# Moving one VectorE product from turn 7 to turn 6 in a fused Mamba and mixture-of-experts layer

## The chip, the cores and the metric

The kernel runs on one core of a Trainium2 chip, in one launch. The metric is the device time in microseconds, the median of several executions. All data is float32.

## The reference

Input x has 2 sequences of 2048 tokens with 256 features. Two blocks follow each other, each on a layer norm of its input and with a residual:

```python
x = x + _L0_attn_ref(_layernorm(x), ...)   # Mamba, then a gated feed-forward of 1024/2
x = x + _L0_ffn_ref(_layernorm(x), ...)    # 8 experts of rank 128, the best 2 of each token count
```

The first holds a state-space scan with 512 channels and 16 states, `h = h * dA + dt * B * x`, `y = sum over states of h * C`. The second, which the change touches:

```python
rw, selected_experts = jax.lax.top_k(routing_weights, TOP_K)
...
combine = jnp.sum(jax.nn.one_hot(selected_experts, N_EXPERTS) * rw[..., None], axis=1)
for e in range(N_EXPERTS):
    out = out + combine[:, e, None] * (x @ Wa[e] @ Wb[e])
```

## The kernel before, in words

The 4096 tokens are cut into 16 tiles of 256 tokens, called steps here and numbered 0 to 15 in their order: (c, b) is chunk c of sequence b, and the two sequences alternate. Each step goes through five stages: `enter` (first norm, input projection, convolution of 4 taps), `ready` (step sizes dt, B and the scan's inputs), `main` (the scans over 16 states), `back` (gate, output projection, feed-forward) and `tail` (router and experts). The stages of different steps are laid over each other: one iteration has 16 turns, one for each state s of the step that is in `main`; around it, in the same turn s, every other stage does its own piece s for another step. So one iteration works on up to five steps, and a step's tail runs two iterations after its scans. The code of all five engines is written in this one order by `drive` (line 147): in a turn first `main(s, n, 0)`, then the four stage functions in an order given for each engine, then `main(s, n, 1)`. Each engine runs its own list in order, and semaphores hold it where it needs another. An opening and a closing list do the turns for which there is no whole iteration; the iterations whose scans are those of chunks 2 to 5 are a loop of two iterations a round.

`main` on VectorE (line 964): `main(s, n, 0)` makes two scans of 128 x 256 (line 975), `main(s, n, 1)` the other two. They read dA (from ScalarE, line 796), psx (PSUM, filled by TensorE from bxT at line 1184) and the state before. GpSimd multiplies the four results with C (hC, line 570), and TensorE sums them over the states in PSUM (line 1203), two turns later. psx has three banks, so TensorE's fill for (turn s + 1, first half) must wait for the scans of (turn s - 1, second half), and a fill of a second half for the scans of (turn s, first half).

The experts in `tail`: the combine weights `cw` become `cT` by a TensorE transpose (line 1297) and a ScalarE copy (line 878, turn 5). SyncE stores cT to DRAM (line 446) and loads it back onto all 128 partitions as `cbc`, 8 experts x 256 tokens (line 450, 1 MB written). TensorE's `hidden(i)` (lines 1320 to 1329) makes x @ Wa of experts 2i and 2i + 1 in the PSUM tile pst, in turns 6, 7, 8 and 9; it waits for the product before, since pst holds one pair. VectorE multiplies this pair by its weights in place, in cbc (line 1031), in turns 7, 8, 9 and 10, and counts `hE_done`. Turns 12 to 14 make the product with Wb. The first product waits for the landing of cbc.

Other work near these turns. VectorE: in turn 6 the output projection's residual x1 and its statistics (lines 991, 907, 912) and two taps of the convolution (line 948, four instructions, `enter`), in turn 7 the last tap (two instructions); in turn 8 `sp_l` (line 956) and `sp_e` (958) of the softplus, in turn 9 its line 962, from which GpSimd makes dt (line 542) and then adds the convolution's edge to `acc` (line 534); ScalarE makes `xc` from it (line 701), then the silu of `sz` (823) and the second gate `yg` (809), for which TensorE waits in turn 10. GpSimd: in turn 6 xn (line 510), in turn 7 nx (line 483), which TensorE transposes in turn 8 (line 1054, called from 1241). TensorE in turn 7 also makes the gate inputs (line 1158), which wait for the last tap.

Steps 12 and 13 have their tails in the iterations where no new step enters, so no taps lie in these turns; steps 14 and 15 have theirs in the closing.

Of the kernel before, what the change touches and what calls it, by code (L numbers as in the profile page):

```python
# [52 lines left out]
def count(per_step, step, k):  # L53

    c, b = step
    value = c * (2 * per_step) + (per_step * b + k)
    return max(value, 0) if isinstance(value, int) else value
# [53 lines left out]
def opening():  # L111

    a, b = (0, 0), (0, 1)

    def turns(stage, step, *at):
        return [(stage, s, step) for s in at]

    return (turns("enter", a, *range(11), 13, 14, 15) + turns("ready", a, 0, 1, 2) + turns("enter", a, 11, 12)
            + turns("ready", a, 5, 6) + turns("enter", b, 0, 1, 2, 3) + turns("ready", a, 7, 8)
            + turns("enter", b, 4) + turns("ready", a, 9) + turns("enter", b, 5) + turns("ready", a, 10)  # L120
            + turns("enter", b, 6, 7, 8, 9, 10) + turns("ready", a, 12, 13, 14, 15)
            + turns("enter", b, 11, 12, 13, 14, 15))


def closing():

    a, b = (NC - 1, 0), (NC - 1, 1)

    def turns(stage, step, *at):
        return [(stage, s, step) for s in at]  # L130

    return (turns("back", b, 0, 1) + turns("tail", a, 0, 1) + turns("back", b, 2, 3) + turns("tail", a, 2, 3)
            + turns("back", b, 4) + turns("tail", a, 4, 5) + turns("back", b, 5, 6, 7)
            + turns("tail", a, 6, 7, 8, 9, 10) + turns("back", b, 8, 9, 10, 11) + turns("tail", a, 12)
            + turns("back", b, 12, 13, 14) + turns("tail", a, 13, 14, 15) + turns("back", b, 15)
            + turns("tail", b, *range(S)))
# [10 lines left out]
def drive(eng, order, enter, ready, main, back, tail):  # L147

    def iteration(t, k, n, r, e):
        stages = {"enter": (enter, e), "ready": (ready, r), "back": (back, k), "tail": (tail, t)}
        for s in range(S):
            if n:
                main(s, n, 0)
            for name in order[s] if s in order else order["else"]:
                stage, step = stages[name]
                if step:
                    stage(s, step)  # L160
            if n:
                main(s, n, 1)

    def pair(c):
        iteration((c - 1, 0), (c - 1, 1), (c, 0), (c, 1), (c + 1, 0))
        iteration((c - 1, 1), (c, 0), (c, 1), (c + 1, 0), (c + 1, 1))

    stages = {"enter": enter, "ready": ready, "back": back, "tail": tail}
    for name, s, step in opening():
        stages[name](s, step)  # L170
    iteration(None, None, (0, 0), (0, 1), (1, 0))
    iteration(None, (0, 0), (0, 1), (1, 0), (1, 1))
    pair(1)
    with eng.Fori(2, NC - 2) as c:
        pair(c)
    pair(NC - 2)
    iteration((NC - 2, 0), (NC - 2, 1), (NC - 1, 0), (NC - 1, 1), None)
    iteration((NC - 2, 1), (NC - 1, 0), (NC - 1, 1), None, None)
    for name, s, step in closing():
        stages[name](s, step)  # L180


def mamba_moe(nc, x, params, w_in, w_x, w_dt, w_out, w_ff, w_fo, w_a, w_b, w_r, bc_scratch, cw_scratch, out):
# [9 lines left out]
    with ctx:  # L193
# [156 lines left out]
        def tail_fill(name, m):  # L350
            units = LAST_TAIL_UNITS if is_last(m) else TAIL_UNITS
            return count(len(units), m, units.index(name) + 1)
# [11 lines left out]
        def wa_bank(i, m):  # L364
            return (psx[0], psx[1], psx[2], psf)[i] if is_late(m) else pst
# [518 lines left out]
        def _(dve):  # L884
# [13 lines left out]
            def link(which, m, ins):  # L898

                chain, per = chains[which]  # L900
                links[which] = links[which] % per + 1
                ins.then_inc(chain, 1)
                dve.wait_ge(chain, count(per, m, links[which]))
# [105 lines left out]
            def tail(s, m):  # L1009
                b = m[1]  # L1010
                if s == 2:
                    dve.wait_ge(filled_tail, tail_fill("rt", m))
                    dve.wait_ge(rn_done, count(1, m, 1))
                    for j in range(SUB):
                        last = nc.vector.tensor_scalar(lg[:, j, :], pst[:, 0, j * NE:(j + 1) * NE], rn[:, j:j + 1], None,
                                                       ALU.mult)
                    last.then_inc(lg_done, 1)
                    dve.wait_ge(lg_done, count(1, m, 1))
                    link("tail", m, nc.vector.reduce_max(mx[:, :], lg[:, :, :], X))
                    nc.vector.tensor_tensor(lgm[:, :, :], lg[:, :, :], mx[:, :].unsqueeze(2).to_broadcast([P, SUB, NE]),  # L1020
                                            ALU.subtract).then_inc(lgm_done, 1)
                if s == 4:
                    dve.wait_ge(psel_done, count(1, m, 1))
                    link("tail", m, nc.vector.reduce_sum(den[:, :], psel[:, :, :], X))
                    nc.vector.reciprocal(rden[:, :], den[:, :]).then_inc(rden_done, 1)
                if s in (7, 8, 9, 10):
                    i = s - 7
                    dve.wait_ge(filled_tail, tail_fill(f"wa{i}", m))
                    if i == 0:
                        dve.wait_ge(cbc_loaded, count(16, m, 16))  # L1030
                    nc.vector.tensor_tensor(cbc[:, 2 * i:2 * i + 2, :], cbc[:, 2 * i:2 * i + 2, :],  # L1031
                                            wa_bank(i, m)[:, :, :], ALU.mult).then_inc(hE_done, 1)
                if s == 15:

                    dve.wait_ge(filled_tail, tail_fill("wb", m))
                    nc.vector.tensor_tensor(x2[:, b], x2[:, b], pst[:, :, :], ALU.add).then_inc(fin_done, 1)

            drive(dve, {"else": ("back", "tail", "ready", "enter")}, enter, ready, main, back, tail)

        @block.tensor  # L1040
        def _(pe):
# [338 lines left out]
```

## Time and profile before

| | |
|---|---|
| median of 3 runs | 1344.15 us (1343.28 to 1348.33) |
| the profiled execution, its own time | 1344.57 us |
| its span | 1342.8 us, 24275 instructions |
| mean granted TensorE clock | 0.982 of full |
| busy TensorE / VectorE / ScalarE / GpSimd | 1225.4 / 999.9 / 1038.2 / 1085.2 us |
| chain that ended last | PE 66%, DVE 9%, issue 5%, ACT 5%, DMA 4%, POOL 2% |

In the profile PE is TensorE's matmuls, PEld its weight loads, DVE VectorE, ACT ScalarE, POOL GpSimd, SP or SPq SyncE with its DMA queue. L1031 is line 1031 of the kernel. Busy time is what an engine's instructions took; "idle before" is the time an engine stood before an instruction, and behind `<-` is what ended it. Instructions of one engine overlap by up to 0.1 us, so that in a run of them the starts count.

### The profile page before, as it was taken

How to read it: one execution, taken by the hardware profiler on the slowest of the kernel's cores; microseconds unless marked ns; L12 is line 12 of the kernel's file. 1: busy time of each engine (PE TensorE's matmuls, PEld its weight loads, DVE VectorE, ACT ScalarE, POOL GpSimd, SP SyncE). 2: the span in 40 equal slices, each digit the busy share in tenths (PEclk: the TensorE clock that was granted, in tenths of full speed). 3: DMA queues.
4: the chain of work that ended last, by engine and by line, in shares of the span. 5: the costliest groups of instructions: out<-in, count | busy, mean ns of one | idle time of the engine just before them, and what ended most of it. 6: DMA issues, size and time to landing. Idle time of an engine off the chain costs nothing.

```text
span 1342.8 us, 24275 instructions
## 1 busy us (share of the span) xinstructions
PE 1225.4 (91%) x7680; PEld 1053.2 (78%) x7680; DVE 999.9 (74%) x1781; ACT 1038.2 (77%) x2505; POOL 1085.2 (81%) x826
## 2 busy tenths in 40 slices
PE   4586889999999999999999999999999999998986
PEld 3365778887878888788888878788887888887875
DVE  2487979778786977879697787969788796878521
ACT  3789888788777978878787887879798787878320
POOL 3389899898888988888898988888898987889621
PEclk8889999999999999999999999999999999999998
DMA  1411111121121111112111121212021021211001
GB/s 66 174 48 41 47 31 66 41 74 47 39 80 45 60 41 53 61 49 80 50 56 41 60 66 36 80 48 69 28 80 48 32 72 48 72 48 64 17 32 48
DMA packets 29223, 75.08 MB, mean 56 GB/s; under 512 B 3104, under 2 KB 15776, under 8 KB 26528
## 3 DMA queue, kind: packets, MB, share of 16 engines
q1 hardware_dynamic: 29088, 73.41, 16.4%
q8 instruction: 69, 1.13, 0.3%
q14 instruction: 66, 0.54, 0.1%
HBM read 64.61 MB, written 4.59 MB: 52 GB/s over the span
## 4 chain that ended last, share of the span: by engine, by line
PE 66%; DVE 9%; issue 5%; ACT 5%; DMA 4%; POOL 2%; DVEq 0%; ACTq 0%; SPq 0%; POOLq 0%
PE psx L1184 11%; PE psy L1203 11%; PE pst L1067 8%; PE psb L1061 7%; PE psb L1067 7%; DVE h L975 4%; PE pst L1061 4%; PE psf L1061 3%; DMA cbc<-cw_scratch 3%; PE psf L1152 2%; PE psf L1104 2%; PE psf L1093 2%; PE psb L1158 2%; PE psf L1158 1%; ACT dA L796 1%
## 5 line engine op out<-in xcount | busy, mean ns | idle before, releaser
L975 DVE TENSOR_TENSOR_SCAN h<-dA,state,psx 128x256 f32<-128x256 f32 x1024 | 682.5, 727 | 114.9 <-PE psx L1184 95.2
L570 POOL TENSOR_TENSOR hC<-h,bC 128x1024 f32<-128x1024 f32 x256 | 606.5, 2373 | 86.7 <-DVE h L975 79.8
L796 ACT ACTIVATE dA<-dt,neg_a 128x256 f32<-128x256 f32 x1024 | 434.2, 499 | 0.0
L1184 PE MATMUL psx<-ident,bxT 128*128 128x128 f32 x2048 | 305.4, 275 | 27.9 <-DVE h L975 17.1
L1184 PEld LDWEIGHTS psx<-ident,bxT 128*128 128x128 f32 x2048 | 244.5, 142 | 70.4 <-issue 24.9
L784 ACT ACTIVATE bxT<-uTs,BT 128x512 f32<-128x512 f32 x352 | 232.6, 715 | 67.4 <-PE psx L1184 65.9
L1203 PE MATMUL psy<-ident,hC 128*128 128x128 f32 x2048 | 265.5, 273 | 1.5 <-POOL hC L570 1.5
L1203 PEld LDWEIGHTS psy<-ident,hC 128*128 128x128 f32 x2048 | 233.1, 142 | 4.7 <-POOL hC L570 1.7
L554 POOL TENSOR_TENSOR bxT<-uTs,BT 128x1024 f32<-128x1024 f32 x80 | 151.9, 1899 | 26.0 <-PE psx L1184 26.0
L1061 PE MATMUL psb<-nT,w_ff_sb 128*128 128x256 f32 x496 | 121.8, 388 | 12.8 <-ACT yg L809 11.2
L1061 PE MATMUL pst<-eT,w_a_sb 128*128 128x256 f32 x448 | 108.9, 386 | 20.4 <-DVE cbc L1031 20.4
L1061 PEld LDWEIGHTS psb<-nT,w_ff_sb 128*128 128x128 f32 x496 | 89.3, 190 | 34.8 <-ACT yg L809 17.5
L1067 PE MATMUL pst<-w_b_sb,cbc 128*128 128x256 f32 x480 | 110.8, 379 | 0.0
L1061 PEld LDWEIGHTS pst<-eT,w_a_sb 128*128 128x128 f32 x448 | 82.6, 192 | 33.4 <-DVE cbc L1031 22.2
L1067 PEld LDWEIGHTS pst<-w_b_sb,cbc 128*128 128x128 f32 x480 | 90.1, 190 | 11.7
L483 POOL TENSOR_SCALAR nx<-x,mv,rstd 128x256 f32<-128x256 f32 x64 | 77.6, 1222 | 24.4 <-ACT rstd L657 24.4
L948 DVE SCALAR_TENSOR_TENSOR acc<-psf,par,acc 128x255 f32<-128x255 f32 (+1 forms) x180 | 73.9, 474 | 26.2 <-ACT halo L696 26.2
L1067 PE MATMUL psb<-w_out_sb,yg 128*128 128x256 f32 x256 | 63.4, 391 | 2.0 <-ACT yg L836 2.0
L1061 PE MATMUL psf<-uT,w_in_sb 128*128 128x256 f32 x240 | 60.2, 395 | 4.5 <-ACT uT L681 2.5
L542 POOL TENSOR_TENSOR dt<-dt,sp_l 128x1024 f32<-128x1024 f32 x16 | 37.8, 2361 | 30.2 <-DVE sp_l L962 30.2
L803 ACT ACTIVATE state<-h 128x4 f32<-128x4 f32 x256 | 50.5, 203 | 13.3 <-DVE h L975 13.3
L1067 PE MATMUL psb<-w_fo_sb,yg 128*128 128x256 f32 x256 | 60.4, 379 | 0.0
(148 smaller groups left out, 1578.8 us busy)
## 6 DMA issues: line engine op xcount, KB each, us to landing
bC<-bc_scratch SPq DMA_DIRECT2D x64, 512.0 KB, 3.9
cbc<-cw_scratch SPq DMA_DIRECT2D x16, 1024.0 KB, 4.8
xf<-in_x SPq DMA_DIRECT2D x16, 256.0 KB, 2.7
xk<-xn SPq DMA_DIRECT2D x16, 256.0 KB, 4.3
xb<-in_x SPq DMA_DIRECT2D x16, 256.0 KB, 4.3
out<-x SPq DMA_DIRECT2D x16, 256.0 KB, 2.2
w_in_sb<-in_w_in SPq DMA_DIRECT2D x1, 1024.0 KB, 5.1
w_ff_sb<-in_w_ff SPq DMA_DIRECT2D x1, 1024.0 KB, 5.9
```

The source lines that it names most:

```text
L483: last = nc.gpsimd.tensor_scalar(dst[:, j, :], src[:, j, :], mv[k][:, j, 0:1], rstd[k + 1][:, j:j + 1], ALU.subtract, ALU.mult)
L554: nc.gpsimd.tensor_tensor(bxT[:, ring(s)], uTs[:, n[1]], BT[:, n[1], :, s:s + 1].to_broadcast([P, SUB, DI]), ALU.mult).then_inc(bxT_pool, 1)
L570: nc.gpsimd.tensor_tensor(hC[:, s % RC], h[:, ring(s)], bC[:, g % RINGG, s % G:s % G + 1, :].to_broadcast([P, NJ, T]), ALU.mult).then_inc( ...
L784: last = nc.scalar.activation(bxT[:, ring(s), j, :], uTs[:, n[1], j, :], ACT.Copy, scale=BT[:, n[1], j, s:s + 1])
L796: last = nc.scalar.activation(dA[:, s % RA, j, :], dt[:, n[1], j, :], ACT.Exp, scale=neg_a[:, j, s:s + 1])
L803: nc.scalar.activation(state[:, n[1], :, s:s + 1], h[:, ring(s), :, T - 1:T], ACT.Copy).then_inc(state_saved, 1)
L948: nc.vector.scalar_tensor_tensor(out=acc[:, j, tap:], in0=x_bank(i, m)[:, j % 2, 0:T - tap], scalar=pcol(C_CONVW + j * TAPS + k), in1=acc[ ...
L975: last = nc.vector.tensor_tensor_scan(h[:, r, j, :], dA[:, s % RA, j, :], psx[bx_bank(fill)][:, k, :], state[:, b, j, s:s + 1], ALU.mult, ...
L1061: last = mm(dst[:, i, :], w[:, k, c:c + P], rhs[:, k, :], start=k == 0, stop=k == kt - 1)
L1067: last = mm(dst[:, j, :], lhs[:, k, j * P:(j + 1) * P], w[:, k, :], start=k == 0, stop=k == kt - 1)
L1184: last = nc.tensor.transpose(psx[bx_bank(fill)][:, k, j * P:(j + 1) * P], bxT[:, ring(s), j, c:c + P], ident[:, :])
L1203: last = mm(psy[j][:, i * P:(i + 1) * P], hC[:, s % RC, i, j * P:(j + 1) * P], ident[:, :], is_transpose=True, start=False, stop=s == S - ...
```

## The change

VectorE makes the product of the first pair (i = 0) in turn 6, and there as the last of the four stages: behind the two taps of `enter` and ahead of `main(6, n, 1)`. The other three stay in turns 8, 9 and 10. No other engine's list changes.

```diff
@@ -1023,8 +1023,8 @@
                     dve.wait_ge(psel_done, count(1, m, 1))
                     link("tail", m, nc.vector.reduce_sum(den[:, :], psel[:, :, :], X))
                     nc.vector.reciprocal(rden[:, :], den[:, :]).then_inc(rden_done, 1)
-                if s in (7, 8, 9, 10):
-                    i = s - 7
+                if s in (6, 8, 9, 10):
+                    i = max(s - 7, 0)
                     dve.wait_ge(filled_tail, tail_fill(f"wa{i}", m))
                     if i == 0:
                         dve.wait_ge(cbc_loaded, count(16, m, 16))
@@ -1035,7 +1035,7 @@
                     dve.wait_ge(filled_tail, tail_fill("wb", m))
                     nc.vector.tensor_tensor(x2[:, b], x2[:, b], pst[:, :, :], ALU.add).then_inc(fin_done, 1)
 
-            drive(dve, {"else": ("back", "tail", "ready", "enter")}, enter, ready, main, back, tail)
+            drive(dve, {6: ("back", "ready", "enter", "tail"), "else": ("back", "tail", "ready", "enter")}, enter, ready, main, back, tail)
```

On VectorE, in turns 6 and 7 of an iteration in which all stages run. The lines of L975 are the scans (two for a half turn), here with their waits: `bx_filled` is TensorE's fill of psx, `exp_done` ScalarE's dA, `hc_done` GpSimd's hC; `cbc_loaded` is the transfer's landing and `filled_tail` TensorE's `hidden(0)`.

```order
 L948 SCALAR_TENSOR_TENSOR acc<-psf,par,acc 128x254 [waits conv_tap] x2
-L975 SCALAR_TENSOR_TENSOR h<-dA,state,psx 128x256 [waits bx_filled]
-L975 SCALAR_TENSOR_TENSOR h<-dA,state,psx 128x256
-L975 SCALAR_TENSOR_TENSOR h<-dA,state,psx 128x256 [waits state_saved,bx_filled,hc_done,exp_done]
-L975 SCALAR_TENSOR_TENSOR h<-dA,state,psx 128x256
 L1031 TENSOR_TENSOR cbc<-cbc,pst 128x512 [waits cbc_loaded,filled_tail]
+L975 SCALAR_TENSOR_TENSOR h<-dA,state,psx 128x256 [waits bx_filled]
+L975 SCALAR_TENSOR_TENSOR h<-dA,state,psx 128x256
+L975 SCALAR_TENSOR_TENSOR h<-dA,state,psx 128x256 [waits state_saved,bx_filled,hc_done,exp_done]
+L975 SCALAR_TENSOR_TENSOR h<-dA,state,psx 128x256
 L948 SCALAR_TENSOR_TENSOR acc<-psf,par,acc 128x253 [waits conv_tap] x2
```

The product has moved ahead of the four scans of (turn 6, second half) and (turn 7, first half); the last tap, which stood behind the product, stands behind the scans.

On TensorE, in the same turns, before and with the change alike: `hidden(0)`, the fill of psx for the second half of turn 7, the sum over states, the fill for the first half of turn 8, `hidden(1)` and the gate inputs.

```order
L1061 MATMUL pst<-eT,w_a_sb 128x256 [waits cT_done]
L1061 MATMUL pst<-eT,w_a_sb 128x256 x3
L1184 MATMUL psx<-ident,bxT 128x128 [waits scan_done]
L1184 MATMUL psx<-ident,bxT 128x128 x3
L1203 MATMUL psy<-ident,hC 128x128 [waits hc_done]
L1203 MATMUL psy<-ident,hC 128x128 x7
L1184 MATMUL psx<-ident,bxT 128x128 [waits scan_done,bxT_pool]
L1184 MATMUL psx<-ident,bxT 128x128 x3
L1061 MATMUL pst<-eT,w_a_sb 128x256 [waits hE_done]
L1061 MATMUL pst<-eT,w_a_sb 128x256 x3
L1158 MATMUL psf<-w_in_sb,uT 128x512 [waits conv_tap]
```

Nothing moved here. The second fill waits by `scan_done` for the scans that now stand behind the product, and `hidden(1)` behind it by `hE_done` for the product.

## Rows read from the trace of the kernel before

**Rows 1.** The page, busy us (share of the span) x instructions.

```profile
PE 1225.4 (91%) x7680; PEld 1053.2 (78%) x7680; DVE 999.9 (74%) x1781; ACT 1038.2 (77%) x2505; POOL 1085.2 (81%) x826
```

**Rows 2.** Who waited for whom: us in total, times, longest us.

```profile
DVE h L975 <- PE psx L1184: 95.2, 68, 4.6
...
PE pst L1061 <- DVE cbc L1031: 20.4, 14, 2.5
...
DVE cbc L1031 <- DMA cbc<-cw_scratch: 15.8, 6, 7.9
```

**Rows 3.** Order of time, VectorE, step 3: start us, us, instruction, count.

```profile
459.45 1.65 DVE L948 SCALAR_TENSOR_TENSOR acc<-psf,par,acc 128x255 f32<-128x255 f32 x4
461.02 2.65 DVE L975 TENSOR_TENSOR_SCAN h<-dA,state,psx 128x256 f32<-128x256 f32 x4
463.59 0.66 DVE L1031 TENSOR_TENSOR cbc<-cbc,pst 128x512 f32<-128x512 f32 x1
464.17 0.86 DVE L948 SCALAR_TENSOR_TENSOR acc<-psf,par,acc 128x253 f32<-128x253 f32 x2
464.95 2.65 DVE L975 TENSOR_TENSOR_SCAN h<-dA,state,psx 128x256 f32<-128x256 f32 x4
...
468.09 2.66 DVE L956 SCALAR_TENSOR_TENSOR sp_l<-sp_l,ln_one,sp_e 128x1024 f32<-128x1024 f32 x1
```

**Rows 4.** Order of time, TensorE, the same stretch; idle before in brackets.

```profile
459.30 1.89 PE L1061 MATMUL pst<-eT,w_a_sb 128*128 128x256 f32 x8
...
462.45 0.66 PE L1184 MATMUL psx<-ident,bxT 128*128 128x128 f32 x4
464.31 1.99 PE L1061 MATMUL pst<-eT,w_a_sb 128*128 128x256 f32 x8 [1.20 <-DVE cbc L1031]
```

**Rows 5.** Order of time, GpSimd, the same stretch.

```profile
462.56 2.36 POOL L570 TENSOR_TENSOR hC<-h,bC 128x1024 f32<-128x1024 f32 x1 [0.43 <-PE psy L1203]
464.91 2.42 POOL L483 TENSOR_SCALAR nx<-x,mv,rstd 128x256 f32<-128x256 f32 x2
467.30 2.37 POOL L570 TENSOR_TENSOR hC<-h,bC 128x1024 f32<-128x1024 f32 x1
```

**Rows 6.** The transfer of cbc: step 3's issue, and landing of all 16.

```profile
456.48 0.33 SPq L450 DMA_DIRECT2D cbc<-cw_scratch  x1
...
DMA to landing us min/median/max: 4.5/4.8/7.4
```

**Rows 7.** The chain that ended last, step 3, turns 9 and 10.

```profile
474.50 1.82 DVE sp_l L962
...
478.80 0.22 POOL acc L534
...
481.14 0.53 ACT yg L809
...
481.71 1.99 PE psb L1061 x8
```

**Rows 8.** Order of time, VectorE, in steps 2, 4 and 13.

```profile
384.52 0.69 DVE L1031 TENSOR_TENSOR cbc<-cbc,pst 128x512 f32<-128x512 f32 x1 [1.17 <-DMA cbc<-cw_scratch]
...
389.44 1.44 DVE L956 SCALAR_TENSOR_TENSOR sp_l<-sp_l,ln_one,sp_e 128x1024 f32<-128x1024 f32 x1
...
542.54 0.69 DVE L1031 TENSOR_TENSOR cbc<-cbc,pst 128x512 f32<-128x512 f32 x1 [0.28 <-DMA cbc<-cw_scratch]
...
547.07 2.26 DVE L956 SCALAR_TENSOR_TENSOR sp_l<-sp_l,ln_one,sp_e 128x1024 f32<-128x1024 f32 x1
...
1231.98 0.69 DVE L1031 TENSOR_TENSOR cbc<-cbc,pst 128x512 f32<-128x512 f32 x1 [2.60 <-DMA cbc<-cw_scratch]
```

**Rows 9.** Windows: us, busy PE, PEld, DVE, ACT, POOL (x), PEclk, DMA share, GB/s.

```profile
385.30:390.60 5.30, 5.30 (x13) 3.54 (x14) 5.03 (x8) 0.48 (x2) 4.04 (x3) 0.68 0.00 0
...
1232.70:1238.00 5.30, 5.28 (x34) 4.89 (x35) 5.30 (x9) 3.02 (x7) 5.03 (x4) 1.00 0.04 5
```

**Rows 10.** Order of time, TensorE, step 13: the transposes of nx.

```profile
1236.30 0.60 PE L1054 MATMUL psb<-ident,nx 128*128 128x128 f32 x4
```

## The prediction

> **What bounds the kernel now.** I read the page first, then the waits, then the order of time on three engines through one pass of turns 6 to 8, and last the chain of waits. The page gives TensorE 1225.4 us, 91% of the span, and no other engine over 81% [rows 1]: TensorE sets the pace where nothing holds it. The list of waits shows what the change is about: TensorE stood still 20.4 us in 14 waits for VectorE's product of line 1031, and VectorE stood still 15.8 us in 6 such products, waiting for the transfer that fills `cbc` [rows 2].
>
> One pass (the one about 460 us) in detail. VectorE ends the taps of turn 6, starts the four scans of (turn 6, second half) and (turn 7, first half) at 461.02, then the product at 463.59, the taps at 464.17, four scans at 464.95, behind them the second product and line 956 at 468.09; there is no idle time between them [rows 3]. I call S the start of those first four scans (461.02). TensorE ends `hidden(0)` at 459.30 + 1.89 = 461.19, fills psx for the next turn at 462.45, which needs the first two of those scans, and starts `hidden(1)` at 464.31 = S + 3.29, 0.72 behind the product's start, after 1.20 of idling [rows 4]. GpSimd runs hC, nx, hC without a gap [rows 5].
>
> So the change's promise is 1.20 us on TensorE in each pass, and its risk is the scans. Two facts decide. First, the transfer: `cbc` is issued at 456.48 and such a transfer lands 4.5 to 7.4 us later, 4.8 in the median [rows 6], that is at about 461.28, while VectorE reaches the new place at S = 461.02. Second, the chain: in this pass it goes through VectorE's line 962 at 474.50, GpSimd's `acc` at 478.80 and ScalarE's `yg` at 481.14 (behind its `xc` and `sz`) to TensorE's matmul at 481.71 [rows 7]. VectorE's time in turns 7 to 9 is therefore on the path, beside TensorE's, and not cover.
>
> **The change part by part.** Nothing is added or removed: the same 16 products at about 0.66 us, no DMA moves, no queue but VectorE's changes order. One product per token step moves ahead of four scans, so VectorE's work is the same in amount; what changes is where it waits, and what is queued behind the wait. Before, the scans ran while the transfer landed. Now they are behind it. Let P be the product's new start: the later of the landing and the end of `hidden(0)` (461.19), so at least S + 0.2. Behind it: scans at P + 0.58 (464.17 - 463.59 [rows 3]), the first two done at about P + 1.95, TensorE's fill, and `hidden(1)` 0.44 later at P + 2.42. VectorE reaches line 956 at P + 7.07, where it was at S + 7.07.
>
> *TensorE's path*: `hidden(1)` moves from S + 3.29 to P + 2.42, that is by (P - S) - 0.87: earlier by up to 0.67, later if the transfer is late.
>
> *VectorE's path*: everything behind moves by P - S, at least 0.2 later. To this comes line 956, whose length depends on GpSimd: it took 1.44 us where GpSimd had finished its hC, 2.26 in between, and 2.66 where hC ran to 467.30 + 2.37 = 469.67, so 1.58 into it [rows 3, 5, 8]. hC of turn 6 now starts with the later scans, at P + 2.1, and the nx and hC behind it end at P + 9.3, so 2.2 us of line 956 run beside GpSimd, and I put it at 1.44 + 2.2 x (1.22 / 1.58) = 3.1 us, 0.45 more than in the usual pass.
>
> The Trainium skill (SBUF — State Buffer, "Who interferes with whom") says that a VectorE instruction with two SBUF inputs contends with a GpSimd instruction that reads SBUF, and that the loser is blocked fully. By that rule line 956 would lose all 2.2 us and take 3.6, and the sum would be some 6 us higher; the row of 2.66 shows 1.22 lost in 1.58, so I stay with the trace.
>
> Nine usual passes (the products of steps 0, 1, 3, 5, 6, 7, 9, 10 and 11; the product was on time in each). P - S, from each step's rows of issue (like 456.48) plus the median 4.8, less its scan row (like 461.02), is 0.75, 0.2, 0.28, 0.26, 1.1, 2.1, 0.2, 0.43 and 0.4: 5.7 us together. Nine times 0.45 for line 956 is 4.0. VectorE's path has no room in the pass shown (the chain passes from one to the next without a wait for anything else [rows 7]) and up to 0.2 in five others, say 1.0 off. **Sum 8.7.**
>
> Three passes whose product already waited or barely made it (steps 2, 4, 8, with line 948 in them). Step 4's product starts at 542.54 after 0.28 of idling for the transfer, step 2's at 384.52 after 1.17 [rows 8]; P is the same before and after, so the four scans (2.57 us) that hid the transfer now come after it. Less room of 0.3 to 0.5 and with line 956 longer by 0.85, that is 2.9 for step 4, and 2.9 for step 8 the same way. In step 2 TensorE's clock had fallen behind that wait (0.68 of full speed, `hidden(1)` and the matmuls behind it at half of the 2.4 GHz for a while [rows 9]), which already cost the step 1.7, so only 1.3 is left. **Sum 7.1.**
>
> Steps 12 and 13, near the end, have no taps. There too the product waits for the transfer, 2.60 us in step 13 [rows 8], and the scans are now behind it. `hidden(1)` moves from P + 0.74 to P + 2.42; in step 12 another 0.5 comes from the fill behind line 956: 2.2. In step 13 TensorE's transposes of nx stood at 1236.30 = P + 4.32 [rows 10] and nx is now ready at P + 6.9: 2.6. **Sum 4.8.** Steps 14 and 15 (the closing) have no scans between turns 6 and 7: 0.
>
> *The clock*: TensorE's gap before the fill becomes P - S + 0.5, which is 3.2 to 4.4 us in steps 2, 4, 8, 12 and 13. A gap of 2.47 dropped the granted clock to half in step 2 and an equal one did not in step 13, where it stayed 1.00 [rows 9]. Each further drop costs at most what it cost in step 2, 1.7, partly covered by the 0.9 that TensorE's path now has to spare. Bounds 0 and 5 x 1.7 = 8.5; I take 1.5, nearer the lower end, since only one of the two gaps fell.
>
> Total: 8.7 + 7.1 + 4.8 + 1.5 = 22.1 us. The profiled execution took 1344.57, 0.4 above the median of the runs, so the forecast is 1344.6 + 22.1 = **1366.7 us**, 1.6% slower. A measurement of this kernel can tell about 0.5%, 6.7 us, from no change.
>
> **The rivals.** *A: VectorE's path has more room than I read, and only TensorE's counts.* Then nine passes give 5.7 - 9 x 0.87 = -2.1, three give 3 x (2.42 - 0.74) = 5.0 and the last two 3.4: +6.3, or 1350.9 us. For it: the room of up to 0.5 in some passes, and TensorE's own path ends level with ScalarE's at 481.71. Against: the chain of the pass shown runs over VectorE, and line 962 feeds GpSimd directly.
>
> *B, faster: the transfer is there when VectorE comes, and TensorE's wait goes.* If P - S is 0.2 in all 14 passes and TensorE's path alone decides, each gains 0.67: 14 x 0.67 = 9.4, or 1335.2 us. It decides from the point where the landing comes less than 0.87 behind S. For it: in seven of the nine usual passes the landing is that near. Against: five of 14 land 2.7 us or more behind S, as their waits show, and VectorE's path loses in every one.
>
> *C: the clock falls in most of the long gaps, and late landings pile up.* The five at 1.7 each and two more landings at 7 us instead of 4.8 give 22.1 + 7 + 5 = +34, or 1379 us. For it: the gaps are longer than the one that fell. Against: an equal gap stayed at full speed.
>
> *D: the place does not matter*, because a later wait swallows either sign, for one that of the scans for psx, 95.2 us in 68 waits [rows 2], which has time to give: 1344.6. Against: the waits lie behind the point where the two paths meet, with TensorE busy throughout.
>
> **How the numbers follow.** Forecast 0.64, A 0.13, B 0.05, C 0.12, D 0.06. The range leaves out B, D, 0.03 of A and half of C, 0.20 in all: 1349 to 1377. Slower by over 0.5% (above 1351.3) are the forecast, C and 0.05 of A: 0.81. Same: D and 0.08 of A, 0.14. Faster: B, 0.05.
>
> **What would show it.** Right: VectorE's wait for `cbc<-cw_scratch` at line 1031 grows from 15.8 us in 6 waits to about 35 in 14 or more; TensorE's wait at `hidden(1)` for line 1031 goes, and a wait of psx for VectorE's scans takes its place; line 956's mean rises from 2.36 us toward 3. Wrong: the landings come before VectorE; or line 956 stays at 2.66 and `acc` of line 534 no later than before against TensorE, which would be A.

## The result and the profile after

The changed kernel takes 1370.63 us in the median of 4 runs (1369.11 to 1372.81), the kernel before 1344.44: 26 us more. The ratio on record is 1.0188, with a 95% interval of 1.0164 to 1.0212; the recorded ratios, here and below, differ from those of the medians by up to 0.001. The forecast was 1366.7 us in a range of 1349 to 1377. The direction and the size held; two steps of the reasoning did not, and part of the size was luck. All three are named below.

| | before | after |
|---|---|---|
| profiled execution's span | 1342.8 us | 1368.9 us |
| mean granted TensorE clock | 0.982 | 0.975 |
| busy TensorE / VectorE | 1225.4 / 999.9 us | 1234.3 / 1009.7 us |
| line 956, mean | 2.36 us | 2.92 us |

The list of waits of the changed kernel (us in total, times, longest us), against [rows 2]:

```profile
POOL hC L570 <- DVE h L975: 109.6, 67, 4.7
DVE h L975 <- PE psx L1184: 94.4, 68, 4.8
...
PE psx L1184 <- DVE h L975: 54.7, 47, 4.4
...
DVE cbc L1031 <- DMA cbc<-cw_scratch: 31.2, 15, 7.7
```

And the first of these in the kernel before:

```profile
POOL hC L570 <- DVE h L975: 79.8, 61, 3.2
```

TensorE's wait for the product at `hidden(1)` (20.4 us in 14 waits) is gone from the list. In its place TensorE's fill of psx waits 54.7 us for the scans, a wait that had 17.1 us before. VectorE's wait for the transfer doubled, from 15.8 us in 6 waits to 31.2 in 15. GpSimd's wait for the scans grew by 29.8 us, about as much as the kernel; the experiments below bear out that the time goes there.

Step 3 again, in order of time. VectorE, against [rows 3]:

```profile
461.76 1.65 DVE L948 SCALAR_TENSOR_TENSOR acc<-psf,par,acc 128x255 f32<-128x255 f32 x4
464.46 0.69 DVE L1031 TENSOR_TENSOR cbc<-cbc,pst 128x512 f32<-128x512 f32 x1 [1.05 <-DMA cbc<-cw_scratch]
465.06 2.65 DVE L975 TENSOR_TENSOR_SCAN h<-dA,state,psx 128x256 f32<-128x256 f32 x4
467.63 0.84 DVE L948 SCALAR_TENSOR_TENSOR acc<-psf,par,acc 128x253 f32<-128x253 f32 x2
...
471.54 3.27 DVE L956 SCALAR_TENSOR_TENSOR sp_l<-sp_l,ln_one,sp_e 128x1024 f32<-128x1024 f32 x1
```

TensorE, against [rows 4]; the last row is the matmul of turn 10 that waits for `yg`:

```profile
461.61 1.89 PE L1061 MATMUL pst<-eT,w_a_sb 128*128 128x256 f32 x8
...
466.50 0.66 PE L1184 MATMUL psx<-ident,bxT 128*128 128x128 f32 x4 [1.69 <-DVE h L975]
466.99 1.89 PE L1061 MATMUL pst<-eT,w_a_sb 128*128 128x256 f32 x8
...
485.74 1.56 PE L1061 MATMUL psb<-nT,w_ff_sb 128*128 128x256 f32 x6 [0.97 <-ACT yg L809]
```

GpSimd, against [rows 5]:

```profile
466.61 2.37 POOL L570 TENSOR_TENSOR hC<-h,bC 128x1024 f32<-128x1024 f32 x1 [2.11 <-DVE h L975]
468.96 2.44 POOL L483 TENSOR_SCALAR nx<-x,mv,rstd 128x256 f32<-128x256 f32 x2
471.36 2.38 POOL L570 TENSOR_TENSOR hC<-h,bC 128x1024 f32<-128x1024 f32 x1
```

The product is where the order says, and VectorE idles 1.05 us ahead of it for the landing. TensorE's matmul of turn 10 stood 17.40 us behind `hidden(1)` (464.31 to 481.71) and now stands 18.75 behind it (466.99 to 485.74). GpSimd's first hC waits 2.11 us for the scans that the product held, where it idled 0.43 before, and nx and the second hC follow it without a gap. Line 956 takes 3.27 us instead of 2.66. Two parts can be told apart here: the wait for the landing, and the product's own 0.6 us, which now also lies ahead of the scans that GpSimd's hC needs.

Where the 26.1 us of span went is read from the times at which SyncE issues the transfer of cbc, one in each step. After, steps 0, 12 and 13:

```profile
223.14 0.33 SPq L450 DMA_DIRECT2D cbc<-cw_scratch  x1
...
1174.48 0.32 SPq L450 DMA_DIRECT2D cbc<-cw_scratch  x1
...
1250.97 0.33 SPq L450 DMA_DIRECT2D cbc<-cw_scratch  x1
```

And before:

```profile
222.21 0.33 SPq L450 DMA_DIRECT2D cbc<-cw_scratch  x1
...
1155.32 0.32 SPq L450 DMA_DIRECT2D cbc<-cw_scratch  x1
...
1227.24 0.33 SPq L450 DMA_DIRECT2D cbc<-cw_scratch  x1
```

Ahead of the first issue 0.9 us came up, in steps 0 to 11 it was 951.3 against 933.1, so 18.2; in step 12 76.5 against 71.9, 4.6; and from step 13 to the end 117.9 against 115.6, 2.4.

### The profile page after: what moved, and what is told of

Its sections match the earlier page's. It is cut to its first block, busy times and chain, and to the rows that moved or that the text cites. A ratio compares the mean times of both kernels' runs of the same rounds, so it can differ in the third digit from the quotient of the medians.

```text
span 1368.9 us, 24275 instructions
## 1 busy us (share of the span) xinstructions
PE 1234.3 (90%) x7680; PEld 1059.2 (77%) x7680; DVE 1009.7 (74%) x1781; ACT 1039.8 (76%) x2505; POOL 1086.6 (79%) x826
## 4 chain that ended last, share of the span: by engine, by line
PE 55%; DVE 12%; ACT 11%; issue 8%; DMA 7%; POOL 3%; DVEq 0%; ACTq 0%; SPq 0%; POOLq 0%
PE psx L1184 10%; PE psy L1203 9%; PE pst L1067 8%; DVE h L975 7%; PE psb L1061 6%; DMA cbc<-cw_scratch 5%; PE psb L1067 5%; ACT dA L796 4%; PE pst L1061 3%; DMA cw_scratch<-cT 2%; PE psf L1152 2%; ACT bxT L784 2%; PE psf L1093 2%; PE psb L1158 2%; PE psf L1104 2%
## 5 line engine op out<-in xcount | busy, mean ns | idle before, releaser
L975 DVE TENSOR_TENSOR_SCAN h<-dA,state,psx 128x256 f32<-128x256 f32 x1024 | 682.4, 726 | 115.6 <-PE psx L1184 94.4
L1184 PE MATMUL psx<-ident,bxT 128*128 128x128 f32 x2048 | 307.6, 276 | 65.7 <-DVE h L975 54.7
L1061 PE MATMUL pst<-eT,w_a_sb 128*128 128x256 f32 x448 | 112.5, 396 | 0.0
L1061 PEld LDWEIGHTS pst<-eT,w_a_sb 128*128 128x128 f32 x448 | 85.8, 199 | 10.8
```

Of the source, the lines that this page charges most:

```text
L975: last = nc.vector.tensor_tensor_scan(h[:, r, j, :], dA[:, s % RA, j, :], psx[bx_bank(fill)][:, k, :], state[:, b, j, s:s + 1], ALU.mult, ...
L1061: last = mm(dst[:, i, :], w[:, k, c:c + P], rhs[:, k, :], start=k == 0, stop=k == kt - 1)
L1184: last = nc.tensor.transpose(psx[bx_bank(fill)][:, k, j * P:(j + 1) * P], bxT[:, ring(s), j, c:c + P], ident[:, :])
```

## The experiments

All times are medians. The kernel before ran beside each group, at 1344.81 us in the first, 1344.88 in the second and 1345.45 in the third. In each text of expectations, "theory" is the prediction's account as the runs up to then had left it, and "rival" what would speak against it. A trace shows one execution of each kernel.

**split_before and split_after: the landing alone.** The transfer of cbc is cut, and the first product waits for the first part:

```diff
-                    sp.dma_start(cbc[:, :, :], cw_scratch.partition_broadcast(P)).then_inc(cbc_loaded, 16)
+                    sp.dma_start(cbc[:, 0:2, :], cw_scratch[0:2, :].partition_broadcast(P)).then_inc(cbc_first, 16)
+                    sp.dma_start(cbc[:, 2:NE, :], cw_scratch[2:NE, :].partition_broadcast(P)).then_inc(cbc_loaded, 16)
...
                     if i == 0:
-                        dve.wait_ge(cbc_loaded, count(16, m, 16))
+                        dve.wait_ge(cbc_first, count(16, m, 16))
+                    if i == 1:
+                        dve.wait_ge(cbc_loaded, count(16, m, 16))
```

SyncE also waits for the first part of the step before. On the kernel before:

> The kernel before, but the transfer of cbc cut in two: experts 0 and 1 (256 KB) first, on a semaphore of their own for which the first product waits, the other six behind it. Estimate for the first part's landing: 2.9 us after the issue instead of 4.8 (the xf rows of 256 KB show 2.7). Theory (a late landing costs time wherever VectorE reaches it first, also before the change): the five waits of before go or shrink by 1.9 each, steps 2, 4 and 8 by 3.5 together with the clock drop of step 2, steps 12 to 15 by 1.9 each: about 1333 to 1337 us. Rival (the waits of before lie beside TensorE's work and cost nothing): 1344.

1339.87 us, a ratio of 0.9959 (0.994 to 0.9978). So a late landing does cost time in the kernel before, 5 us; that is less than the 7 to 11 expected. The first part landed 3.7 us behind its issue in the median, not at the 2.9 of the estimate. On the changed kernel:

> The changed kernel with the same cut transfer, so that the landing is no longer what the product waits for in turn 6; it starts as soon as hidden(0) is done, 0.2 us behind VectorE. Theory (the loss is the landing in the larger part, and in the smaller part VectorE's path, 0.2 us later and with line 956 longer by 0.5 beside GpSimd's hC): most of the 26 us come back, but it stays slower than the kernel before with the same cut by 0.5 to 0.7 us in 12 passes and 2 in steps 12 and 13: about 1344, 10 above split_before. Rival (the landing is the whole loss, and TensorE then gains its 0.67 us in each pass): 8 us below split_before, about 1327.

1354.88 us, a ratio of 1.0074 (1.0049 to 1.0098). The earlier landing takes 15.8 of the 26 us back (1370.6 less 1354.9). With the same cut on both sides, the move still costs 15.0 us, not 10, and is far from the rival's gain of 8. Of these 15.0 a part is still the landing. In steps 0 to 11 of split_after no product waits for the transfer, so what is lost there has another cause. In steps 12 and 13 the expectation that the landing is out of the way fails; there the products still wait for it:

```profile
1165.83 0.69 DVE L1036 TENSOR_TENSOR cbc<-cbc,pst 128x512 f32<-128x512 f32 x1 [3.29 <-DMA cbc<-cw_scratch]
...
1240.32 0.69 DVE L1036 TENSOR_TENSOR cbc<-cbc,pst 128x512 f32<-128x512 f32 x1 [4.12 <-DMA cbc<-cw_scratch]
```

In split_before these two waits are 0.84 and 1.32 us. The run split_main below tells the two groups of steps apart. In step 3 of split_after TensorE starts `hidden(1)` at 464.77 and the matmul behind `yg` 18.74 us later:

```profile
464.28 0.65 PE L1189 MATMUL psx<-ident,bxT 128*128 128x128 f32 x4 [0.77 <-DVE h L978]
464.77 1.46 PE L1066 MATMUL pst<-eT,w_a_sb 128*128 128x256 f32 x6
...
483.51 1.99 PE L1066 MATMUL psb<-nT,w_ff_sb 128*128 128x256 f32 x8 [0.96 <-ACT yg L812]
```

Against the issue of cbc in this step (457.26 here, 453.77 in split_before), `hidden(1)` came at 7.51 instead of 7.82, so TensorE did gain 0.3; and the matmul in turn 10 came at 26.25 instead of 25.23, so 1.0 later. The early start buys nothing.

**between: the product behind two scans instead of none.** Called for the tail's step once `main(6, n, 1)` is done:

```diff
             if n:
                 main(s, n, 1)
+            if behind and t and s == 6:
+                behind(t)
```

> The first product behind main(6, n, 1), so behind two of the four scans of the change: only the two scans of (turn 7, first half) stand behind the wait, TensorE's next fill of psx does not. Theory: the landing is there in eight of nine usual passes, line 956 is as long as before (2.66 us, mean 2.4), VectorE's path is not shorter, so TensorE's 1.2 us are not gained except for the 0.2 of room in some passes; steps 2, 4 and 8 lose up to 1.3 each: 1344 to 1349. Rival (TensorE's wait for the product is on the path by itself): 1.2 us in nine passes, 1334.

1344.08 us, 0.9992 (0.9972 to 1.0012): no change, as expected, and not the 10 us that TensorE's wait would be worth. The products of steps 14 and 15 stay where they were. In its step 3 `hidden(1)` starts at 458.76, 6.55 us behind the issue of cbc, where the kernel before has 7.83. The matmul behind `yg` starts at 25.19, where it has 25.23:

```profile
452.21 0.33 SPq L452 DMA_DIRECT2D cbc<-cw_scratch  x1
...
458.76 1.35 PE L1066 MATMUL pst<-eT,w_a_sb 128*128 128x256 f32 x5
...
477.40 0.92 PE L1066 MATMUL psb<-nT,w_ff_sb 128*128 128x256 f32 x3 [0.96 <-ACT yg L811]
```

So in this step the wait that the change was to remove, 1.2 us, was worth nothing: TensorE ran into the next one, for `yg`, that much earlier (0.69 us of idling there became 0.96, 0.41 went in a wait for scans in turn 9, and the rest in shorter ones). The median alone would not show it, for it holds a loss of another kind, which the expectation did not have: the products of steps 12 and 13 wait 3.12 and 3.54 us for the transfer, and from the issue of step 12 to the end this trace has 191.1 us against 187.5 in the kernel before. The run between_split below gives what the place is worth in steps 0 to 11.

**pad_before: is VectorE's list in turn 7 on the path?** One memset that nothing reads, behind the first product:

```diff
+                    if i == 0 and not is_late(m):
+                        nc.vector.memset(idle[:, :], 0.0)
```

> The kernel before with one memset of 128x512 on VectorE behind the first product of steps 0 to 13, about 0.5 us each by estimate, nothing reads it. Theory (VectorE's turns 7 to 9 are on the path with no room in most passes): 12 passes with 0.3 to 0.5 us each, 4 to 6 us slower, about 1349. Rival A of the prediction (VectorE has room): 1344.4.

1344.92 us, 1.0004 (0.9984 to 1.0024). The theory was wrong here: 14 times 0.485 us on VectorE cost nothing that can be measured. The trace shows why. Step 3 of pad_before, VectorE and then GpSimd:

```profile
461.03 0.48 DVE L1036 MEMSET idle<- 128x512 f32 x1
...
465.24 2.23 DVE L958 SCALAR_TENSOR_TENSOR sp_l<-sp_l,ln_one,sp_e 128x1024 f32<-128x1024 f32 x1
```

```profile
464.01 2.37 POOL L572 TENSOR_TENSOR hC<-h,bC 128x1024 f32<-128x1024 f32 x1
```

Line 956 (958 here) starts later, 12.20 us behind the issue of cbc instead of 11.61, but is shorter, 2.23 us instead of 2.66, and ends at 467.47, 1.09 us behind the end of GpSimd's hC (466.38). In the kernel before it is 470.75 against 469.67, 1.08, and in the changed one 474.81 against 473.74, 1.07. The instruction's end is set by GpSimd's, not by its own start. So the path runs from the scans of turn 6 over GpSimd's hC, nx and hC to line 956, and VectorE's own list has room beside it.

**pad_turn6 and pad_long: the same load ahead of the scans, and more of it behind.** In pad_turn6 the product stays in turn 7, and the memset stands behind the two taps of turn 6, where the change puts the product:

```diff
+                if s == 6 and not is_late(m):
+                    nc.vector.memset(idle[:, :], 0.0)
```

> The kernel before with the same memset of 128x512 (0.485 us each in the run pad_before, where it cost nothing behind the product), now ahead of the scans of (turn 6, second half), at the place where the change puts the product. Theory (what the change delays is not VectorE's own list but GpSimd's hC, nx, hC, which starts with these scans and whose end sets the end of line 956): 0.4 to 0.5 us in each of 12 passes, less some room, about 1349. Rival (a VectorE delay of half a microsecond is absorbed wherever it lies): 1344.5.

1349.18 us, 1.0032 (1.0014 to 1.005). The same 0.485 us, four scans earlier, costs 4.3 us. The intervals of the two runs overlap a little, but the traces tell them apart: from the issue of cbc in step 0 to that in step 12 pad_turn6 takes 935.4 us, pad_before 929.9, and last_two (below), whose steps 0 to 11 are those of the kernel before, 929.6. The traced execution of the kernel before has 933.1 there, about 3 us of it from the late landing in step 2. In turn 6 the memset also delays the product and `hidden(1)`, by half a microsecond; split_after rules this out as the cause, since `hidden(1)` is earlier there and the loss remains. pad_long has four memsets behind the product:

```diff
+                    if i == 0 and not is_late(m):
+                        for k in range(4):
+                            dve.wait_ge(pad_done, count(4, m, k))
+                            nc.vector.memset(idle[:, :], 0.0).then_inc(pad_done, 1)
```

> The kernel before with four memsets of 128x512 in a chain behind the first product of steps 0 to 13, about 2.0 to 2.3 us each time, at the place where one of 0.485 us cost nothing. Theory (VectorE has about 1.0 us of room there, which is the time until GpSimd is done with nx and can begin hC of turn 7): what goes beyond 1.0 us is paid in 12 passes, 12 to 15 us, about 1358; line 956 then starts later and is shorter, but still ends 1.08 us behind hC. Rival (VectorE's list in turn 7 has room for more than 2 us, so the change's loss has nothing to do with it): 1344.5.

1361.32 us, 1.0122 (1.0102 to 1.0142), 15.9 us. In step 3 GpSimd's second hC now waits for VectorE, and line 956 (959 here) ends at 473.81, 1.08 behind it:

```profile
466.37 2.43 POOL L486 TENSOR_SCALAR nx<-x,mv,rstd 128x256 f32<-128x256 f32 x2
470.36 2.37 POOL L573 TENSOR_TENSOR hC<-h,bC 128x1024 f32<-128x1024 f32 x1 [1.55 <-DVE h L978]
```

```profile
465.06 0.67 DVE L1034 TENSOR_TENSOR cbc<-cbc,pst 128x512 f32<-128x512 f32 x1
...
468.16 0.74 DVE L951 SCALAR_TENSOR_TENSOR acc<-psf,par,acc 128x253 f32<-128x253 f32 x2
...
471.97 1.84 DVE L959 SCALAR_TENSOR_TENSOR sp_l<-sp_l,ln_one,sp_e 128x1024 f32<-128x1024 f32 x1
```

The memsets push the taps from 0.58 behind the product's start to 3.10, so by 2.52 us, and 1.55 of it reaches GpSimd: room for 1.0 us. This run is the direct test of the path over GpSimd: once VectorE's list makes GpSimd's second hC late, it costs time.

**ahead_of_taps: the half of the change in the order of stages undone.** Turn 6 keeps its old order, so the product also stands ahead of the two taps:

```diff
-            drive(dve, {6: ("back", "ready", "enter", "tail"), "else": ("back", "tail", "ready", "enter")}, enter, ready, main, back, tail)
+            drive(dve, {"else": ("back", "tail", "ready", "enter")}, enter, ready, main, back, tail)
```

> The changed kernel with turn 6 in the old order of stages, so that the product stands ahead of the two taps too, 1.57 us earlier in VectorE's list. The product cannot start earlier (the landing, and hidden(0), which ends 0.2 us behind VectorE's arrival at the place of the change), so the taps are held as well and the scans come 1.6 us later still. Theory (every microsecond by which the scans of turn 6, second half, come later is paid): 1.5 us more than the change in each of 12 passes, near 1388. Rival (the loss is the landing alone, the same in both): 1370.

1387.23 us, 1.0307 (1.0274 to 1.034), 16.6 more than the change. Twelve times the two taps' 1.57 us would be 18.8, so most of what the product holds behind it is paid. Some of it may be the clock: its mean is 0.961 to 0.972 in these executions, against 0.969 to 0.975 with the change. The rival's 1370 is out.

**last_two and split_main: which steps.** The move for steps 12 and 13 only, without the cut:

```diff
+def moved(step):
+    return isinstance(step[0], int) and step[0] == NC - 2
...
-                if s in (6, 8, 9, 10):
+                if s in (8, 9, 10) or s == (6 if moved(m) else 7):
```

> The move of the change in steps 12 and 13 only, all others as before. The prediction put 4.8 us on these two without the clock. Theory now (from the trace of the change: the granted clock falls to half behind both gaps there): 4.8 and about 1.7 for each drop, 1351 to 1353. Rival (4.8 alone, the drops are covered): 1349.

1349.45 us, 1.0044 (1.0029 to 1.0059): 4.6 us by the medians, near the rival's number, and 3.9 to 7.9 by the interval, which also holds a part of the theory's. The trace speaks for the rival: from the issue of step 12 to the end it has 192.3 us, against 187.5 in the kernel before and in pad_before. That is the prediction's 4.8, although the clock did fall behind both gaps. And the move for steps 0 to 11, with the cut (`moved` is true for all but chunks 6 and 7):

> The changed kernel with the cut transfer, but the move in steps 0 to 11 only; in the others the product is in turn 7. Theory (with the landing out of the way steps 0 to 11 lose 0.5 to 0.7 each by the late start of GpSimd's chain, and steps 12 and 13 the rest of the 15 us between split_after and split_before): 1347 to 1349. Rival (the 15 us lie in steps 0 to 11): 1354.

1348.65 us, 1.0035 (1.0017 to 1.0053). That is 8.8 above split_before, 0.73 a step, and the last two steps hold the other 6.2 of the 15.0. The 0.73 is what the place costs with an early landing. It is close to the sum of the product's own 0.6 us and the wait of up to 0.2 us for `hidden(0)` in front of it. (One product in the trace of split_main, that of step 7, still waits 1.28 us for the transfer.)

**between_split: the two that helped or did no harm together.**

> The product behind main(6, n, 1) and the cut transfer together, the version that might beat both kernels. Theory: no product waits for the landing of more than 0.3 us in steps 0 to 11, GpSimd's chain is as before, TensorE's wait for the product goes but only some 0.2 us of room in five passes is gained by it: 1336 to 1339. Rival (TensorE's wait of 1.2 us for the product is worth something by itself once the landing is early): 1328 or less.

1339.0 us, 0.9963 (0.9948 to 0.9979). It is faster than the kernel before by its interval, and so is split_before; the two can't be told apart. The cut transfer is the gain. Their traces show how little this place is worth even with an early landing: steps 0 to 11 take 928.3 us against 930.2 in split_before, so less than 0.2 us a step of the 1.2 that TensorE had waited, and from step 12 to the end 1.1 us is lost again (186.7 against 185.5), where the products of steps 12 and 13 wait 2.32 and 3.08 us for the transfer.

## Why the prediction was right where it was, and where not

*The new wait.* P - S, the product's start against the old start of the scans, was forecast from issue plus 4.8 us. It held in kind: 15 waits instead of "14 or more", and 31.2 us where "about 35" stood. In single steps the landing scattered: step 2's took 7.4 us before and 4.9 now, and step 8's product waited 3.58 us. The sum was about right, not the steps: the nine usual passes waited 7.6 us in all, where P - S was put at 5.7, and steps 2, 4 and 8 waited 6.2, where the rows give 9.4 (1.17 and 0.28 more than 2.57, and step 8 like step 4). The prediction took the late landing of step 2 for a property of that step; in last_two and pad_before it doesn't occur there.

*TensorE's gain is limited by the two scans behind the product.* This held: `hidden(1)` was forecast at P + 2.42 and came at 2.53 (466.99 less 464.46).

*"VectorE's turns 7 to 9 are on the path, with no room": wrong in its wording.* pad_before shows 0.5 us of VectorE's list there for nothing, pad_long about 1.0. What is on the path begins with the scans of turn 6, second half, and goes over GpSimd. The forecast came out near all the same, and that is luck as far as the path goes: the change delays exactly those scans, by the wait and by the product's own 0.6 us. hC moves from S + 1.54 to P + 2.15 (466.61 less 464.46), the end of line 956 from S + 9.73 to P + 10.35. The prediction counted the second part as 0.45 us of a longer line 956 on VectorE. The chain of waits named line 962 and not GpSimd's hC ahead of it, since the block between the two engines is no semaphore.

*Line 956* was put at 3.1 us by a rate taken from one row, against 3.6 by the Trainium skill's rule (SBUF — State Buffer, "Who interferes with whom": the loser is blocked fully). It measured 3.27. The rule was right and my base wrong: the row of 1.44 already held 0.36 us beside hC (it too ends 1.08 behind it), so the unhindered length is less; in step 12 of split_before, where it began ahead of hC, it took 1.28. With the right base, 1.08 us and all of the 2.20 beside hC, the rule gives 3.28. From 2.66 us at 1.58 beside hC to 3.27 at 2.20 the instruction grew by 0.61 for 0.62 of overlap: blocked fully, not at the 0.77 (1.22 of 1.58) of the prediction. This made the nine usual passes 0.15 us too cheap each.

*The terms.* Steps 0 to 11 were put at 8.7 + 7.1 and measured 18.2, the clock included. Read step by step at the matmul that waits for `yg`, the nine usual passes lost 12.1 us instead of 8.7: their waits were 1.9 longer and line 956 took 1.4 more than forecast. Steps 2, 4 and 8 lost 6.3 instead of 7.1, but as -0.4, 1.2 and 5.5 where 1.3, 2.9 and 2.9 had been put. So two errors of opposite sign stand in the sum, and where the late landings fell was chance. Steps 12 and 13 were put at 4.8 and measured 7.0 in the profiled execution, 4.8 in the trace of last_two.

*The clock.* It was put at 1.5 us over five steps. TensorE's gap in step 8 was 4.21 us, and the granted clock fell behind it, as it did in steps 12 and 13. Windows of the changed kernel (us, busy PE, PEld, DVE, ACT, POOL, PEclk, DMA share, GB/s):

```profile
868.00:872.50 4.50, 4.50 (x12) 3.27 (x12) 4.48 (x9) 2.31 (x6) 4.50 (x4) 0.50 0.00 0
...
1182.00:1187.00 5.00, 5.00 (x13) 3.65 (x12) 4.14 (x7) 2.40 (x6) 5.00 (x4) 0.53 0.02 3
...
1258.30:1263.00 4.70, 4.70 (x22) 3.88 (x21) 4.33 (x8) 3.20 (x8) 4.70 (x4) 0.64 0.00 0
```

```profile
867.30 1.12 PE L1184 MATMUL psx<-ident,bxT 128*128 128x128 f32 x4 [4.21 <-DVE h L975]
868.21 3.62 PE L1061 MATMUL pst<-eT,w_a_sb 128*128 128x256 f32 x8
```

`hidden(1)` took 3.62 us there instead of 1.89, at half of 2.4 GHz. The matmul behind `yg` stood 22.48 us behind the product, where steps 3, 5 and 7 have 21.28 or 21.29, so this drop reached it with 1.2 us; that of step 2 with 0.3 (21.52 against 21.21 in step 4). How much those of steps 12 and 13 cost stays open: in last_two's profiled execution the clock fell behind both gaps as well (0.66 of full in the 5 us behind each), and the rise was the 4.8 us forecast without it, so whether the term was too small is not shown. The 0.9 us ahead of step 0, and 2.1 in split_after against split_before, are not explained either; the clock in the opening differs between executions.

*Rival A* (only TensorE's path counts, 1350.9) fell with split_after, though its room on VectorE's list was real (pad_before). *B* fell with split_after and between, *D* with the result. Of *C* a part came true: the clock fell in four of the five steps named, 2, 8, 12 and 13, behind gaps of 2.27, 4.21, 3.67 and 4.42 us. In step 4 the gap was 1.58.

## What to carry to other kernels

Before moving an instruction up to shorten someone's wait, ask what it must wait for itself at the new place, and what is then queued behind it: here a DMA's landing that four scans had hidden. A wait of 1.2 us in each of many steps can be worth almost nothing if the same engine meets a later one that is set by another chain; moving only the product and not the scans (between) shows it in one run. A pad of half a microsecond at two places in an engine's list tells which part of the list is on the path, where the chain of waits can't.

## What the hardware showed that was not expected

VectorE's line 956, with two inputs in SBUF, ended 1.07 to 1.09 us behind GpSimd's hC whenever it began beside it, for starts from 0.36 to 2.20 us ahead of hC's end, in all four kernels quoted: VectorE is held for the whole rest of hC, and the end of one engine's instruction depends on the other's without any wait in the list.

It also works the other way round. In step 12 of split_before line 956 (959 here) begins 0.63 us ahead of hC:

```profile
1160.46 1.28 DVE L959 SCALAR_TENSOR_TENSOR sp_l<-sp_l,ln_one,sp_e 128x1024 f32<-128x1024 f32 x1
1161.66 2.87 DVE L961 TENSOR_SCALAR sp_e<-sp_e 128x1024 f32<-128x1024 f32 x1
```

```profile
1161.09 2.90 POOL L573 TENSOR_TENSOR hC<-h,bC 128x1024 f32<-128x1024 f32 x1
```

Line 956 takes 1.28 us, hC 2.90 instead of 2.37, and the next instruction of VectorE, which begins while hC runs, 2.87 instead of 0.68. So in these rows the instruction that begins second is the one that is held. split_after shows the same in its step 12.

Cut in two, the 1 MB transfer of cbc has its first 256 KB landed in 3.7 us in the median and the other 768 KB in 5.2, against 4.8 for the whole.
